# A fourth chunk of rotary angles reduced on TensorE, and three steps of the first units in another order

## The chip, the core and the metric

The kernel runs on one core of one Trainium2 chip. The core has TensorE (PE, matrix products into eight PSUM banks), VectorE (DVE), ScalarE (ACT), GpSimd (POOL) and SyncE (SP, which issues DMAs here); each works through its own queue of instructions in order, and semaphores tie the queues together. The metric is the device time of one launch in microseconds (us), the median of the runs. Before the change it is 1221.59 us over 3 runs (1221.35 to 1222.02).

## The reference, cut to what matters

One layer: cross attention with rotary positions over 64 sequences, then a mixture of experts. Only the head of it bears on the change: keys and queries are turned by cosine and sine of position times frequency.

```python
inv_freq = 1.0 / THETA ** (jnp.arange(0, HD, 2, dtype=jnp.float32) / HD)
freqs = pos.astype(jnp.float32)[:, None, :, None] * inv_freq
emb = jnp.concatenate((freqs, freqs), axis=-1)
return x * jnp.cos(emb) + _rotate_half(x) * jnp.sin(emb)
...
q = _rope(_rms_norm(layernorm(x) @ Wq.T), draft_position_ids)      # 16 heads of 128
k = _rope(_rms_norm(concat(ctx, x) @ Wk.T), full_position_ids)     # 4 key heads
probs = softmax(q @ k.T * SCALE); attn = probs @ v; x = x + tanh(g) * (attn @ Wo.T)
x = x + tanh(g2) * (top-2 of 8 experts + shared expert)(layernorm(x))
```

## The kernel before

The 4096 tokens are 32 tiles of 128 tokens (two sequences each). A unit of attention is one tile t and one key head g, n = 4t + g; `pair` in each engine's queue holds the eight units of two tiles, and the pairs run one after another. The first pair is written apart, since the tables of angles and the split weights are made beside it. The order of every engine's queue is the order of the calls in its block, written out by hand; nothing is scheduled.

**Tables of angles.** The angles are made in eight chunks of 128x512, `sincos[c]`, numbers 0 to 3 for context positions and 4 to 7 for token positions (X0 = 4, so X0 + 3 is 7). They are taken in the order 0, 4, 1, 5, 2, 6, 3, 7 (`CHUNKS`). A chunk passes through: position times frequency (VectorE, L1241); the number of whole turns by adding and taking away a rounding constant (`whole_turns` on ScalarE, L927 and L928, or `first_turns` on VectorE); taking the turns back out in three parts of 2 pi, either as three dependent VectorE operations (`turn_back`, L1261) or as four products with scaled identities on TensorE (`angle_left`, L1899 and L1901) that leave the angle in a PSUM bank; the clamp to just below pi (`clamp`, L1275, VectorE, which also reads the PSUM bank); and `tables` on ScalarE: absolute value (L934), sine (L935), cosine as the sine of pi/2 minus the absolute value (L936). `PE_ANGLES` lists the chunks that TensorE turns back, and `b_angle` their banks. The clamps add to the semaphore `angle_v` in the order of `CHUNKS`; each finished table adds to `sin_ready`, on which SP stores the chunk to `trig_scratch`.

**The first units beside it.** TensorE makes the first queries and keys and values (L1814, L1825) from unsplit weights, transposes turned keys and queries (`heads_T`, L1844, L1848), and forms the scores (L1859), for which it needs ScalarE's copy of the transposed queries (`queries_out`, L968) and VectorE's copy of the keys (`keys_out`, L1339). ScalarE takes the sums of squares (`query_squares` L962, `key_squares` L950), copies the values (L957), and forms the exponentials of the scores (L979) after a change of its function table (the load at L1062). GpSimd turns the sums of squares into scales and finishes queries and keys (L767 to L782). VectorE turns keys (`turn_keys`, L1317, L1319) and queries (L1331, L1333).

**The second context tile.** SP loads `ctx_raw` of tile 1 (`load_inputs(1, 1)`, L446) behind the last four loads of query and key weights. `context_hi(1, ...)` on ScalarE (L1002) copies it into `kv_in_hi`; it waits for that load alone. `context_lo(1, 1)` on VectorE takes the remainder later.

```python
            tables(2)
            tables(X0 + 2)
            tables(3)
            query_squares(1, 1)
...
                    if g == 0 and not end:
                        context_hi(t + 1, i + p, 1 - p)
```

Of the kernel before, what the change touches and what calls it, by code (L numbers as in the profile page):

```python
# [24 lines left out]
ALU = mybir.AluOpType  # L25
ACT = mybir.ActivationFunctionType
# [72 lines left out]
def flamingo(nc, x, ctxT, posx, posc, invf, g_xattn, g_ffn, q_w, k_w, wq, wkv, wo, wr, wg, wd, out):  # L99
    ctx = ExitStack()  # L100
    with ctx:
# [64 lines left out]
        def wkv_group(a, g):  # L166
# [56 lines left out]
        X0 = NCH // 2  # L223
        pos_f = sb("pos_f", [P, 2 * TILES], F32, stage_at)
        sincos = [sb(f"sincos{c}", [P, CH, 2, HALF], F32,
                     early_at if c in (0, X0) else stage_at if c == 2 else None) for c in range(NCH)]
# [94 lines left out]
        b_q, b_kv, b_qT, b_kT, b_sc, b_pT, b_aT, b_o = [  # L321
            bank(n) for n in ("b_q", "b_kv", "b_qT", "b_kT", "b_sc", "b_pT", "b_aT", "b_o")]
        b_count = b_table = b_kT
        b_angle = (b_sc, b_pT, b_aT)
        b_sg, b_shT, b_sT, b_sy = [b_q, b_kv], [b_qT, b_sc], [b_kT, b_o], [b_aT, b_pT]
        b_early = (b_q, b_kv, b_pT, b_aT), (b_qT, b_sc, b_pT, b_aT)
        b_gate, b_up, b_down = (b_q, b_kv), (b_kT, b_o), (b_sc, b_qT, b_aT, b_pT)
# [97 lines left out]

        CHUNKS = [c for n in range(X0) for c in (n, X0 + n)]
        ACT_TURNS = [0, X0, 1, X0 + 1, 3, X0 + 3]
        PE_ANGLES = [X0 + 1, 2, X0 + 2]
        turned_at, back_done = {}, {}


# [480 lines left out]
        def _(act):  # L912
# [4 lines left out]
            def step(ins):  # L917

                steps[0] += 1
                ins.then_inc(act_step, 1)  # L920
                act.wait_ge(act_step, steps[0])
# [8 lines left out]
            def tables(c):  # L930

                act.wait_ge(angle_v, CHUNKS.index(c) + 1)
                cos, sin = sincos[c][:, :, 0, :], sincos[c][:, :, 1, :]
                step(nc.scalar.activation(cos, sin, ACT.Abs))  # L934
                nc.scalar.activation(sin, sin, ACT.Sin)  # L935
                nc.scalar.activation(cos, cos, ACT.Sin, bias=half_pi[:], scale=-1.0).then_inc(sin_ready, 1)  # L936

# [115 lines left out]
            whole_turns(X0 + 3)  # L1053
            tables(2)
            tables(X0 + 2)
            tables(3)
            query_squares(1, 1)

# [5 lines left out]
            def pair(i, first, last, part):  # L1064
                for u in range(2 * KVH):
                    p, g = divmod(u, KVH)
# [22 lines left out]
                        split_hi(pieces[2 * u - 2:2 * u])  # L1089
                    if isinstance(i, int) and i == 1 and p == 0:  # L1090
                        split_hi(pieces[SPLITS + g:SPLITS + g + 1])
                    if g == 0 and not end:
                        context_hi(t + 1, i + p, 1 - p)
                    if g == 1 and not end:
                        normed_hi(t + 1, 1 - p)
# [129 lines left out]
        def _(dve):  # L1225
# [29 lines left out]
            def turn_back(*chunks):  # L1255
                for part in TWO_PI:
                    for c in chunks:
                        if part == TWO_PI[0]:
                            dve.wait_ge(turns_ready, ACT_TURNS.index(c) + 1)
                        turn, a = sincos[c][:, :, 0, :], sincos[c][:, :, 1, :]  # L1260
                        link(nc.vector.scalar_tensor_tensor(out=a, in0=turn, scalar=-part, in1=a, op0=ALU.mult,  # L1261
                                                            op1=ALU.add), len(chunks))
                        back_done[c] = steps[0]

            def clamp(*chunks):
                for c in chunks:
                    a = sincos[c][:, :, 1, :]
                    if c in PE_ANGLES:
                        n = PE_ANGLES.index(c)
                        dve.wait_ge(count_done, n + 1)  # L1270
                        left = b_angle[n][:].rearrange("p (t n) -> p t n", t=CH)
                    else:
                        dve.wait_ge(step_v, back_done[c])
                        left = a
                    nc.vector.tensor_scalar(a, left, PI_BELOW, -PI_BELOW, ALU.min, ALU.max).then_inc(angle_v, 1)  # L1275

            pieces = list(enumerate(split_pieces()))
# [198 lines left out]
                                    ALU.mult).then_inc(sin_w_ready, 1)  # L1476
            turn_queries(0, 0, 0, 0)
            clamp(2)
            turn_back(3)
            turn_keys(0, 0, 0)  # L1480
            clamp(X0 + 2, 3)
            turn_back(X0 + 3)
            clamp(X0 + 3)
            dve.wait_ge(st_trig_first, 16 * 2)
            keys_out(0, 0)
# [283 lines left out]
        def _(pe):  # L1769
# [138 lines left out]
            first_keys_values(0)  # L1908
            angle_left(1)
            angle_left(2)  # L1910
            first_queries(1)

            def shared_half(t, j, done):
# [368 lines left out]
```

## Time and profile before

| | us |
|---|---|
| median of 3 runs | 1221.59 |
| the profiled execution | 1223.99 |
| its span, first to last instruction | 1222.2 |
| TensorE busy | 1199.6 (98%) |
| VectorE busy | 1037.9 (85%) |
| GpSimd busy | 941.1 (77%) |
| ScalarE busy | 903.5 (74%) |
| chain that ended last | PE 92%, DVE 4%, ACT 3%, issue 1% |

Busy times are of one profiled execution, and a busy TensorE is not one at its peak. A row of a timeline has the start in us from the start of the span, the time taken, the engine, the line, the operation and the tiles; a bracket at its end tells how long the engine had been idle and what ended that. Buffer numbers are left out of the names there, so all eight chunks read `sincos`. A row of the view of stretches has from:to and length in us, the busy us of PE, PEld (weight loads), DVE, ACT and POOL with their instructions, the clock granted to TensorE as a share of 2.4 GHz, the busy share of the DMA engines, and GB/s.

### The profile page before, as it was taken

How to read it: one execution, taken by the hardware profiler on the slowest of the kernel's cores; microseconds unless marked ns; L12 is line 12 of the kernel's file. 1: busy time of each engine (PE TensorE's matmuls, PEld its weight loads, DVE VectorE, ACT ScalarE, POOL GpSimd, SP SyncE). 2: the span in 40 equal slices, each digit the busy share in tenths (PEclk: the TensorE clock that was granted, in tenths of full speed). 3: DMA queues.
4: the chain of work that ended last, by engine and by line, in shares of the span. 5: the costliest groups of instructions: out<-in, count | busy, mean ns of one | idle time of the engine just before them, and what ended most of it. 6: DMA issues, size and time to landing. Idle time of an engine off the chain costs nothing.

```text
span 1222.2 us, 31455 instructions
## 1 busy us (share of the span) xinstructions
PE 1199.6 (98%) x8765; PEld 1113.0 (91%) x8766; DVE 1037.9 (85%) x3014; ACT 903.5 (74%) x3774; POOL 941.1 (77%) x1124
## 2 busy tenths in 40 slices
PE   6899999999999999999999999999999999999999
PEld 3788999999999999999999999999999999999887
DVE  8788999999999999999989999988888777777554
ACT  7978787887888778887888877877777646666422
POOL 2778888888888888888888888888888525555585
PEclk9999999999999999999999999999999999999999
DMA  6634233332222222223333333332235636555485
GB/s 178 201 105 127 83 99 104 111 97 90 90 90 90 90 92 93 90 95 94 96 96 114 107 101 99 105 102 80 75 108 151 225 105 192 158 164 159 149 274 183
DMA packets 141079, 148.55 MB, mean 122 GB/s; under 512 B 13824, under 2 KB 124672, under 8 KB 140256
## 3 DMA queue, kind: packets, MB, share of 16 engines
q1 hardware_dynamic: 126096, 125.97, 34.2%
q0 software_dynamic: 6480, 17.77, 4.0%
q10 hardware_dynamic: 8448, 4.20, 1.2%
q8 instruction: 21, 0.34, 0.1%
q14 instruction: 34, 0.28, 0.1%
HBM read 66.93 MB, written 80.76 MB: 121 GB/s over the span
## 4 chain that ended last, share of the span: by engine, by line
PE 92%; DVE 4%; ACT 3%; issue 1%; DMA 0%; SPq 0%; DVEq 0%; ACTq 0%
PE b_kv L1801 14%; PE b_q L1787 14%; PE b_o L1885 13%; PE b_sc L1859 9%; PE b_aT L1874 9%; PE b_pT L1867 5%; PE b_qT L1848 4%; PE b_q L2121 3%; PE b_kv L2121 3%; PE b_kT L1844 2%; PE b_kT L2181 1%; PE b_o L2181 1%; PE b_kv L2181 1%; PE b_q L2181 1%; PE b_aT L2138 1%; PE b_pT L2138 1%
## 5 line engine op out<-in xcount | busy, mean ns | idle before, releaser
L1801 PE MATMUL b_kv<-w_group,kv_in_hi 128*128 128x256 f32 x992 | 204.9, 304 | 0.0
L979 ACT ACTIVATE probs<-b_sc,neg_max 128x128 f32<-128x128 f32 x512 | 180.6, 371 | 2.6 <-DVE neg_max L1343 2.1
L773 POOL TENSOR_TENSOR q_rot<-q_rot,q_sin 128x512 f32<-128x512 f32 x128 | 176.7, 1381 | 7.2 <-DVE q_sin L1333 2.4
L769 POOL TENSOR_TENSOR qk_r<-qk_me,minus_half 128x6 f32<-128x6 f32 x128 | 172.0, 1344 | 10.1
L1801 PEld LDWEIGHTS b_kv<-w_group,kv_in_hi 128*128 128x128 f32 x992 | 161.3, 190 | 7.3 <-issue 0.4
L1787 PE MATMUL b_q<-w_group,kv_in_hi 128*128 128x512 f32 x496 | 164.8, 413 | 0.4 <-DVE q_sin L1333 0.4
L1885 PE MATMUL b_o<-wo_hi,aT_hi 128*128 128x256 f32 x480 | 143.5, 299 | 0.3 <-DVE aT_lo L1357 0.3
L1859 PE MATMUL b_sc<-kT,qT 128*128 128x128 f32 x1024 | 136.3, 276 | 6.2 <-ACT qT L968 4.5
L776 POOL TENSOR_TENSOR q_rot<-q_rot,qk_r 128x512 f32<-128x512 f32 x128 | 133.7, 1044 | 10.0
L1801 PE MATMUL b_kv<-w_group,kv_in_lo 128*128 128x256 f32 x496 | 139.6, 282 | 0.0
L962 ACT ACTIVATE junk<-b_q 128x128 bf16<-128x128 f32 x512 | 134.0, 283 | 0.0
L1874 PE MATMUL b_aT<-pT,v 128*128 128x256 f32 x512 | 133.9, 384 | 0.0
L1859 PEld LDWEIGHTS b_sc<-kT,qT 128*128 128x128 f32 x1024 | 125.0, 191 | 8.8 <-issue 7.6
L1885 PE MATMUL b_o<-wo_lo,aT_hi 128*128 128x256 f32 x480 | 132.9, 277 | 0.0
L1885 PE MATMUL b_o<-wo_hi,aT_lo 128*128 128x256 f32 x480 | 132.7, 276 | 0.0
L973 ACT ACTIVATE pT<-b_pT 128x512 f32<-128x512 f32 x128 | 76.8, 600 | 69.6 <-PE b_pT L1867 67.6
L767 POOL TENSOR_TENSOR qk_me<-qk_ms,eps_rms 128x6 f32<-128x6 f32 x128 | 32.2, 252 | 108.6 <-ACT junk L950 108.4
L962 ACT ACTIVATION_READ_ACCUMULATOR junk<-b_q 128x1 f32 x512 | 111.2, 217 | 0.0
L1343 DVE TENSOR_REDUCE neg_max<-b_sc 128x4 f32<-128x512 f32 x128 | 88.0, 688 | 24.0 <-PE b_sc L1859 22.8
L979 ACT ACTIVATION_READ_ACCUMULATOR probs<-b_sc,neg_max 128x1 f32 x512 | 108.0, 211 | 0.0
L1874 PEld LDWEIGHTS b_aT<-pT,v 128*128 128x128 f32 x512 | 94.2, 189 | 15.0 <-issue 0.5
L782 POOL TENSOR_TENSOR k_rot<-k_rot,k_sin 128x256 f32<-128x256 f32 x128 | 94.6, 739 | 6.0 <-DVE k_sin L1319 4.3
(332 smaller groups left out, 3977.3 us busy)
## 6 DMA issues: line engine op xcount, KB each, us to landing
xs_scratch<-zeros SPq DMA_DIRECT2D x34, 1032.0 KB, 6.2
s_in<-xs_scratch SPq DMA_DIRECT2D x71, 129.0 KB
yT_scratch<-yT SPq DMA_DIRECT2D x32, 256.0 KB
routed<-ys_scratch SPq DMA_DIRECT2D x32, 256.0 KB, 4.3
w_hi_all<-w_scratch SPq DMA_DIRECT2D x3, 1536.0 KB, 14.4
x_in<-in_x SPq DMA_DIRECT2D x32, 128.0 KB, 2.3
ctx_raw<-in_ctxT SPq DMA_DIRECT2D x32, 128.0 KB, 2.5
trig_scratch<-sincos SPq DMA_DIRECT2D x8, 512.0 KB, 5.9
```

The costliest lines, as they stand in the source:

```text
L769: nc.gpsimd.tensor_tensor(qk_r[g % 2][:], qk_me[:], minus_half[:, 0:REP + NB], ALU.pow).then_inc(r_ready, 1)
L773: nc.gpsimd.tensor_tensor(q_rot[g % 2][:], q_rot[g % 2][:], q_sin[g % 2][:], ALU.add) \
L776: nc.gpsimd.tensor_tensor(q_rot[g % 2][:], q_rot[g % 2][:], qk_r[g % 2][:, 0:REP].unsqueeze(2).to_broadcast([P, REP, HD]), ALU.mult) \
L782: nc.gpsimd.tensor_tensor(k_rot[g % 2][:], k_rot[g % 2][:], k_sin[g % 2][:], ALU.add) \
L962: last = nc.scalar.activation(junk[:, h, :], b_q[:, h * HD:(h + 1) * HD], ACT.Square, scale=HD ** -0.5, accum_out=qk_ms[g % 2][:, h:h + 1])
L979: last = nc.scalar.activation(probs[:, j, :], b_sc[:, j * P:(j + 1) * P], ACT.Exp, bias=neg_max[g % 2][:, j:j + 1], accum_out=row_sum[g % ...
L1343: nc.vector.tensor_reduce(neg_max[g % 2][:], b_sc[:].rearrange("p (j n) -> p j n", j=REP), AX.X, ALU.max, negate=True).then_inc(max_ready, 1)
L1787: last = nc.tensor.matmul(b_q[:], kv_in[p][a][:, c, 1:3, :], wq_of(b, gg)[:, c, :], start=(c == 0 and (a, b) == PASSES[0]), stop=(c == DC ...
L1801: last = nc.tensor.matmul(b_kv[:, s * 2 * HD:(s + 1) * 2 * HD], kv_in[p][a][:, c, 2 * s:2 * s + 2, :], wkv_of(b, c)[:, g % KVH, :], start= ...
L1859: last = nc.tensor.matmul(b_sc[:, o:o + P], qT[:, s, 2 * j:2 * j + 2, :], kT[:, s, :], start=True, stop=True)
L1874: last = nc.tensor.matmul(b_aT[:, s * REP * S:(s + 1) * REP * S], v_s[g % KVH][:, s, :], pT[:, s, :], start=True, stop=True)
L1885: last = nc.tensor.matmul(b_o[:, 0:D], aT[a][:, h, :, :], wo_s[b][:, gg * REP + h, :], start=(gg == 0 and h == 0 and (a, b) == PASSES[0]), ...
```

## The change

Five edits. Chunk 3 joins the chunks that TensorE turns back, with bank `b_o`; its three VectorE operations go. `angle_left(3)` is put behind `angle_left(2)` and ahead of the queries of unit 1. On VectorE, the keys of unit 0 are turned right behind the clamp of chunk 2, and the clamp of chunk 3 comes behind the turning back of chunk 7. The absolute value of chunk 7 goes from ScalarE to VectorE. The context copy of tile 1 is taken out of unit 0 and put between the tables of chunks 6 and 3.

```diff
--- before.py
+++ after.py
@@ -321,7 +321,7 @@
         b_q, b_kv, b_qT, b_kT, b_sc, b_pT, b_aT, b_o = [
             bank(n) for n in ("b_q", "b_kv", "b_qT", "b_kT", "b_sc", "b_pT", "b_aT", "b_o")]
         b_count = b_table = b_kT
-        b_angle = (b_sc, b_pT, b_aT)
+        b_angle = (b_sc, b_pT, b_aT, b_o)
         b_sg, b_shT, b_sT, b_sy = [b_q, b_kv], [b_qT, b_sc], [b_kT, b_o], [b_aT, b_pT]
         b_early = (b_q, b_kv, b_pT, b_aT), (b_qT, b_sc, b_pT, b_aT)
         b_gate, b_up, b_down = (b_q, b_kv), (b_kT, b_o), (b_sc, b_qT, b_aT, b_pT)
@@ -425,7 +425,8 @@
 
         CHUNKS = [c for n in range(X0) for c in (n, X0 + n)]
         ACT_TURNS = [0, X0, 1, X0 + 1, 3, X0 + 3]
-        PE_ANGLES = [X0 + 1, 2, X0 + 2]
+        PE_ANGLES = [X0 + 1, 2, X0 + 2, 3]
+        DVE_ABS = [X0 + 3]
         turned_at, back_done = {}, {}
 
 
@@ -931,7 +932,8 @@
 
                 act.wait_ge(angle_v, CHUNKS.index(c) + 1)
                 cos, sin = sincos[c][:, :, 0, :], sincos[c][:, :, 1, :]
-                step(nc.scalar.activation(cos, sin, ACT.Abs))
+                if c not in DVE_ABS:
+                    step(nc.scalar.activation(cos, sin, ACT.Abs))
                 nc.scalar.activation(sin, sin, ACT.Sin)
                 nc.scalar.activation(cos, cos, ACT.Sin, bias=half_pi[:], scale=-1.0).then_inc(sin_ready, 1)
 
@@ -1053,6 +1055,7 @@
             whole_turns(X0 + 3)
             tables(2)
             tables(X0 + 2)
+            context_hi(1, 0, 1)
             tables(3)
             query_squares(1, 1)
 
@@ -1089,7 +1092,7 @@
                         split_hi(pieces[2 * u - 2:2 * u])
                     if isinstance(i, int) and i == 1 and p == 0:
                         split_hi(pieces[SPLITS + g:SPLITS + g + 1])
-                    if g == 0 and not end:
+                    if g == 0 and not (end or first and p == 0):
                         context_hi(t + 1, i + p, 1 - p)
                     if g == 1 and not end:
                         normed_hi(t + 1, 1 - p)
@@ -1272,6 +1275,9 @@
                     else:
                         dve.wait_ge(step_v, back_done[c])
                         left = a
+                    if c in DVE_ABS:
+                        nc.vector.scalar_tensor_tensor(out=sincos[c][:, :, 0, :], in0=left, scalar=-1.0, in1=left, op0=ALU.mult,
+                                                       op1=ALU.max)
                     nc.vector.tensor_scalar(a, left, PI_BELOW, -PI_BELOW, ALU.min, ALU.max).then_inc(angle_v, 1)
 
             pieces = list(enumerate(split_pieces()))
@@ -1476,10 +1482,10 @@
                                     ALU.mult).then_inc(sin_w_ready, 1)
             turn_queries(0, 0, 0, 0)
             clamp(2)
-            turn_back(3)
             turn_keys(0, 0, 0)
-            clamp(X0 + 2, 3)
+            clamp(X0 + 2)
             turn_back(X0 + 3)
+            clamp(3)
             clamp(X0 + 3)
             dve.wait_ge(st_trig_first, 16 * 2)
             keys_out(0, 0)
@@ -1908,6 +1914,7 @@
             first_keys_values(0)
             angle_left(1)
             angle_left(2)
+            angle_left(3)
             first_queries(1)
 
             def shared_half(t, j, done):
```

ScalarE, from the tables of chunk 2 to the change of function table; sincos_138, 142, 139, 143 are chunks 2, 6, 3, 7. Before:

```order
L936 ACTIVATE sincos_142<-sincos_142,half_pi 128x8x64
L934 ACTIVATE sincos_139<-sincos_139 128x8x64
L935 ACTIVATE sincos_139<-sincos_139 128x8x64
L936 ACTIVATE sincos_139<-sincos_139,half_pi 128x8x64
L962 ACTIVATE junk,qk_ms_107<-b_q 128x128 x4
L968 ACTIVATE qT<-b_qT 128x4x2x64
L950 ACTIVATE junk,qk_ms_107<-b_kv 128x128 x2
L934 ACTIVATE sincos_143<-sincos_143 128x8x64
L935 ACTIVATE sincos_143<-sincos_143 128x8x64
L936 ACTIVATE sincos_143<-sincos_143,half_pi 128x8x64
L957 ACTIVATE v_120<-b_kv 128x256
L1002 ACTIVATE kv_in_hi<-ctx_raw_96 128x2x2x64
```

ScalarE, the same stretch in the changed kernel:

```order
L938 ACTIVATE sincos_142<-sincos_142,half_pi 128x8x64
L1004 ACTIVATE kv_in_hi<-ctx_raw_96 128x2x2x64
L936 ACTIVATE sincos_139<-sincos_139 128x8x64
L937 ACTIVATE sincos_139<-sincos_139 128x8x64
L938 ACTIVATE sincos_139<-sincos_139,half_pi 128x8x64
L964 ACTIVATE junk,qk_ms_107<-b_q 128x128 x4
L970 ACTIVATE qT<-b_qT 128x4x2x64
L952 ACTIVATE junk,qk_ms_107<-b_kv 128x128 x2
L937 ACTIVATE sincos_143<-sincos_143 128x8x64
L938 ACTIVATE sincos_143<-sincos_143,half_pi 128x8x64
L959 ACTIVATE v_120<-b_kv 128x256
```

The context copy has moved ten instructions forward, ahead of the tables of chunk 3, and one absolute value of chunk 7 is gone.

VectorE, behind the turning of the first queries (`sincos_138<-b_pT` is the clamp of chunk 2). Before:

```order
L1275 TENSOR_SCALAR sincos_138<-b_pT 128x8x64
L1261 SCALAR_TENSOR_TENSOR sincos_139<-sincos_139 128x8x64 x3
L1317 SCALAR_TENSOR_TENSOR k_rot_115<-b_kv,qk_r_109,cos_w_85 128x128
L1319 SCALAR_TENSOR_TENSOR k_sin_117<-b_kv,qk_r_109,sin_w_87 128x128
L1317 SCALAR_TENSOR_TENSOR k_rot_115<-b_kv,qk_r_109,cos_w_85 128x128
L1319 SCALAR_TENSOR_TENSOR k_sin_117<-b_kv,qk_r_109,sin_w_87 128x128
L1275 TENSOR_SCALAR sincos_142<-b_aT 128x8x64
L1275 TENSOR_SCALAR sincos_139<-sincos_139 128x8x64
L1261 SCALAR_TENSOR_TENSOR sincos_143<-sincos_143 128x8x64 x3
L1275 TENSOR_SCALAR sincos_143<-sincos_143 128x8x64
```

VectorE, the same stretch in the changed kernel:

```order
L1281 TENSOR_SCALAR sincos_138<-b_pT 128x8x64
L1323 SCALAR_TENSOR_TENSOR k_rot_115<-b_kv,qk_r_109,cos_w_85 128x128
L1325 SCALAR_TENSOR_TENSOR k_sin_117<-b_kv,qk_r_109,sin_w_87 128x128
L1323 SCALAR_TENSOR_TENSOR k_rot_115<-b_kv,qk_r_109,cos_w_85 128x128
L1325 SCALAR_TENSOR_TENSOR k_sin_117<-b_kv,qk_r_109,sin_w_87 128x128
L1281 TENSOR_SCALAR sincos_142<-b_aT 128x8x64
L1264 SCALAR_TENSOR_TENSOR sincos_143<-sincos_143 128x8x64 x3
L1281 TENSOR_SCALAR sincos_139<-b_o 128x8x64
L1279 SCALAR_TENSOR_TENSOR sincos_143<-sincos_143 128x8x64
L1281 TENSOR_SCALAR sincos_143<-sincos_143 128x8x64
```

Three operations of chunk 3 are gone from in front of the keys' turn, and one on chunk 7 (its absolute value) is new.

## Rows read from the trace of the kernel before

**Rows 1.** Stretches, the steady loop: busy us of five engines, clock, DMA share, GB/s.

```profile
200.00:600.00 400.00, 400.00 (x3063) 376.80 (x3062) 365.27 (x1021) 321.44 (x1464) 343.95 (x386) 1.00 0.31 97
```

**Rows 2.** Timeline of TensorE, 21 to 43 us.

```profile
21.77 1.02 PE L1899 MATMUL b_aT<-sincos,ident 128*128 128x512 f32 x2
22.63 2.74 PE L1901 MATMUL b_aT<-sincos,back 128*128 128x512 f32 x6
25.21 1.88 PE L1814 MATMUL b_q<-wq_raw,kv_first 128*128 128x512 f32 x4
28.36 0.44 PE L1844 MATMUL b_kT<-ident,k_rot 128*128 128x128 f32 x2 [1.27 <-POOL k_rot L782]
...
33.50 1.49 PE L1859 MATMUL b_sc<-kT,qT 128*128 128x128 f32 x8 [2.53 <-ACT qT L968]
34.78 3.24 PE L1814 MATMUL b_q<-wq_raw,kv_first 128*128 128x512 f32 x4
...
39.59 0.38 PE L1844 MATMUL b_kT<-ident,k_rot 128*128 128x128 f32 x2
39.81 0.60 PE L1848 MATMUL b_qT<-ident,q_rot 128*128 128x128 f32 x4
41.43 1.13 PE L1859 MATMUL b_sc<-kT,qT 128*128 128x128 f32 x8 [1.02 <-ACT qT L968]
```

**Rows 3.** Stretches of the head, same columns.

```profile
34.10:37.50 3.40, 3.40 (x9) 1.85 (x8) 1.90 (x6) 3.35 (x6) 3.24 (x4) 0.50 1.01 297
...
41.40:58.00 16.60, 16.57 (x100) 14.49 (x101) 14.47 (x27) 15.65 (x59) 13.19 (x13) 1.00 0.47 151
```

**Rows 4.** The chain that ended last, in order: start, us, what.

```profile
37.75 1.40 ACT probs L979 x8
```

**Rows 5.** Timeline of ScalarE, 28 to 42 us.

```profile
28.13 0.63 ACT L934 ACTIVATE sincos<-sincos 128x512 f32<-128x512 f32 x1 [2.41 <-DVE sincos L1275]
...
29.95 0.61 ACT L934 ACTIVATE sincos<-sincos 128x512 f32<-128x512 f32 x1
...
33.72 0.67 ACT L934 ACTIVATE sincos<-sincos 128x512 f32<-128x512 f32 x1
34.42 0.63 ACT L935 ACTIVATE sincos<-sincos 128x512 f32<-128x512 f32 x1
...
35.57 0.36 ACT L957 ACTIVATE v<-b_kv 128x256 f32<-128x256 f32 x1
35.83 0.40 ACT L1002 ACTIVATE kv_in_hi<-ctx_raw 128x256 fp32r<-128x256 f32 x1
36.25 1.28 ACT L1062 ACT_TABLE_LOAD   x1
...
37.66 0.35 ACT L979 ACTIVATE probs<-b_sc,neg_max 128x128 f32<-128x128 f32 x1
...
40.63 0.66 ACT L968 ACTIVATE qT<-b_qT 128x512 f32<-128x512 f32 x1
```

**Rows 6.** Timeline of VectorE, 23 to 31 us.

```profile
23.25 3.09 DVE L1261 SCALAR_TENSOR_TENSOR sincos<-sincos 128x512 f32<-128x512 f32 x3
...
27.42 0.68 DVE L1275 TENSOR_SCALAR sincos<-b_aT 128x512 f32<-128x512 f32 x1
...
28.51 2.13 DVE L1261 SCALAR_TENSOR_TENSOR sincos<-sincos 128x512 f32<-128x512 f32 x3
```

**Rows 7.** Timeline of GpSimd: scales of unit 0, key sum of unit 1.

```profile
22.75 1.34 POOL L769 TENSOR_TENSOR qk_r<-qk_me,minus_half 128x6 f32<-128x6 f32 x1
...
37.95 0.72 POOL L782 TENSOR_TENSOR k_rot<-k_rot,k_sin 128x256 f32<-128x256 f32 x1
```

**Rows 8.** Timeline of SP: the issue of the second context tile.

```profile
25.24 0.67 SPq L446 DMA_DIRECT2D ctx_raw<-in_ctxT  x1
```

**Rows 9.** DMA issues, 25 to 25.9 us; last number: us to landing.

```profile
ctx_raw<-in_ctxT SPq DMA_DIRECT2D x1, 128.0 KB, 6.8
```

**Rows 10.** Line L446, first 5 us: the first context tile.

```profile
DMA to landing us min/median/max: 2.2/2.2/2.2
```

## Prediction, made before the changed kernel ran

> **What bounds the kernel now.** I read the stretches of the run first. In the steady loop TensorE is busy 400.00 of 400 us and its clock is full [rows 1]. What happens in the first 40 us can therefore reach the end in one way only: by the moment from which TensorE runs without a gap. The timeline of TensorE shows where that is [rows 2]. It waits 1.27 us at 28.36 for the first keys from GpSimd, 2.53 us at 33.50 and 1.02 us at 41.43, both times for ScalarE's copy of the transposed queries (qT). Behind the scores of the second unit at 41.43 it is busy 16.57 of 16.60 us [rows 3]. So the number to forecast is the shift of that 41.43, and every microsecond of it is a microsecond of the kernel.
>
> The chain of waits says what sets 41.43. Ahead of it there is no TensorE, only ScalarE, through the first exponentials at 37.75 in that view [rows 4]. The timeline of ScalarE gives its links [rows 5]: tables of chunk 6 from 28.13 (after an idle 2.41 us, for the clamp on VectorE), tables of chunk 3 from 29.95, sums of squares of unit 1, absolute value of chunk 7 at 33.72 and its sine at 34.42, values at 35.57, the context copy at 35.83, the load of the function table at 36.25, exponentials at 37.66, second qT at 40.63. The 2.41 us of idleness is what the reordered clamps can shorten.
>
> **The change, part by part.**
>
> VectorE, keys before the turning back. The three operations of chunk 3 (3.09 us at 23.25) stand before the keys' turn and the clamp of chunk 6 at 27.42 [rows 6]. Without them the keys can go once GpSimd has their scales, at 22.75 + 1.34 = 24.1 [rows 7], and take the 1.04 us that lie between the end of the three (26.34) and 27.42. The clamp of chunk 6 then needs TensorE's third block, whose last product ends at 22.63 + 2.74 = 25.37 [rows 2]. With its 0.68 us ScalarE can begin chunk 6 at about 26.1 instead of 28.13: 2.0 us earlier. Chunk 6 takes 29.95 - 28.13 = 1.82 us [rows 5], so ScalarE is free at 27.9.
>
> ScalarE, the context copy. It now stands there, and waits for `ctx_raw` of tile 1. SP issues that load at 25.24 [rows 8], and it lands 6.8 us later [rows 9], at 32.04. Nothing in the change comes ahead of that issue: the loads before it wait for chunks 0 and 4 and for weights, which are as before. So ScalarE, free at 27.9, stands for 4.1 us. In the kernel before, the copy ran at 35.83 and found its data there. Queued behind the waiting copy are the tables of chunk 3, the sums of squares of unit 1, the first qT, the tables of chunk 7, the values and the exponentials; for them wait GpSimd's scales of unit 1, VectorE's turn of its queries, and TensorE's first scores. The copy occupies 36.25 - 35.83 = 0.42 us at most, so the tables of chunk 3 begin at 32.04 + 0.4 = 32.45 against 29.95: +2.5 us. That is the large term. The sums of squares, the first qT and the first scores (33.50, now 36.0) take it over whole.
>
> The Trainium skill (DMA: Bandwidth & Descriptors, section Two DMAs through the same engine are not ordered) says that within one queue of one engine descriptors start in order, though their writes may finish out of order. By that rule the 128 KB stand behind the weights issued before them. The trace agrees: 6.8 us here, 2.2 us for the same transfer at the start, with little ahead of it [rows 9, 10].
>
> ScalarE, two things taken away behind that. The absolute value of chunk 7 frees 34.42 - 33.72 = 0.70 us. The context copy is gone from between values and table load; the load then waits for the end of the values' copy (35.57 + 0.36 = 35.93) instead of 36.23, which frees 0.30 us [rows 5]. Together: first exponentials at 37.66 + 2.5 - 0.70 - 0.30, a shift of +1.5 us.
>
> VectorE, the absolute value as a fourth operation on chunk 7, and the late clamp of chunk 3. TensorE's fourth block costs what the third did, 25.21 - 21.77 = 3.44 us [rows 2], and ends at 25.37 + 3.44 = 28.8. VectorE's three operations on chunk 7 take 2.13 us [rows 6] from 26.1, so it waits for the block and clamps chunk 3 until 29.5. The absolute value (0.7 us, as one of the three) and the last clamp end near 30.7. Cost zero: ScalarE wants chunk 3 at 32.45. If that cover is gone, chunk 3 can start at 29.5.
>
> TensorE, the fourth block. It pushes the queries of unit 1 to 28.65, and with their 1.88 us the first transposes to about 30.5 instead of 28.36 [rows 2]. The keys of unit 1 end near 33.0 instead of 31.0. All of it lies before the scores at 36.0. Cost zero; without cover 2.1 us, on qT.
>
> From the exponentials to 41.43 there are two ways. By ScalarE alone the second qT moves from 40.63 by +1.5, and the scores to 42.9. It needs the transposes of unit 1 done by 42.1. GpSimd's sum of its keys ran at 37.95 for 0.72 us [rows 7]; it hangs on the sums of squares and moves by 2.5, to end at 41.2, and the transposes take 40.41 - 39.59 = 0.82 us [rows 2]: 42.0, just in time. That holds with TensorE at full clock. Before, it was not: between 34.10 and 37.50 the granted clock was 0.50, so 1.2 GHz, after the idle 2.53 us [rows 3], and the queries of unit 2 took 3.24 us instead of the 1.88 of unit 1 at full clock [rows 2]. That slowness was covered. If it follows the scores again, the distance from scores to transposes stays at 39.59 - 33.50 = 6.09, they start at 42.1, end at 42.9, qT takes 0.66 and TensorE begins about 0.15 later: 43.7, a shift of +2.2. The idle time before the scores is now 3.0 us rather than 2.53, so a fall is no less likely, but TensorE worked longer just before it (until 33.0). I can't decide between the two ends and take the middle.
>
> The sum: +1.5 to +2.2, taken as +1.85 us. The profiled execution took 1223.99 (span 1222.2 and 1.8 around it), 2.4 above the median; the difference is laid on the median: 1221.59 + 1.85 = 1223.4.
>
> **The rivals.**
>
> (a) The load isn't late. If `ctx_raw` lands by 29.2, ScalarE copies it while it waits for the clamp of chunk 3, which ends at 29.5 instead of 29.95: -0.4. With -0.70 and -0.30 that is -1.4 us, 1220.2. The balance is zero for a landing at 30.5. For it: the first context tile took only 2.2 us [rows 10]. Against it: this very transfer took 6.8 [rows 9], and what is ahead of it is unchanged. [...]
>
> (b) Nothing much moves: a landing near 30.5, or losses and gains that meet elsewhere. 1221.6. It needs the load to be 1.5 us faster than in the trace.
>
> (c) Clearly slower: the fall of TensorE's clock comes later and lies on work that nothing covers. The place is behind the second scores, from 42.9 on. A stretch as long as the one before (3.4 us) at half speed costs 1.7 us of full-speed work [rows 3]: 1.5 + 1.7 = +3.2, 1224.8. It decides as soon as the low clock reaches past 42.9. For it: the idle time before the first scores is longer and ends 2.5 us later. Against it: before, the clock was back 4 us after TensorE resumed at 33.50; the same distance now gives 40.0.
>
> A fourth thought, that TensorE's extra block itself sets the pace, needs ScalarE's wait to vanish; then transposes at 30.5 and a chunk 3 at 29.5 would still be in time for qT at 32.3, so it belongs to (a).
>
> **How the numbers follow.** Forecast 0.67, (a) 0.12, (b) 0.08, (c) 0.13. A change of 0.2% (2.4 us) is about what this measurement can tell from none. The forecast's own range, with 0.4 us for run to run, (the three runs spread over 0.67) is 1222.7 to 1224.2; a fifth of it lies above 1224.0, so slower by over 0.2% gets 0.13 of it and all of (c): 0.26. Faster by over 0.2% (under 1219.2) needs more than (a): 0.03. Within 0.2%: 0.71. The range of 8 in 10 takes in (b), (c) and the upper edge of (a): 1220.6 to 1225.0.
>
> **What would show it.** In the profile after: ScalarE idle for about 4 us before the context copy, ended by the DMA of `ctx_raw`, at about 32.1; tables of chunk 6 at 26.1; the table load 1.5 us later than 36.25; TensorE idle some 3 us before scores at 36.0; second scores at 42.9 to 43.7, the upper end only if the granted clock is low over the queries of unit 2; no gap behind that. The forecast is wrong if the copy finds its data (a), if TensorE waits there for anything but qT, or if the shift at 41.43 doesn't reach the end.

## The result

| | before | changed |
|---|---|---|
| median, us (22 runs each) | 1222.03 | 1223.82 |
| lowest to highest | 1221.35 to 1223.24 | 1222.98 to 1225.38 |
| profiled execution, its span | 1223.99, 1222.2 | 1223.86, 1222.1 |
| second scores in the profile | 41.43 | 43.84 |

The ratio of changed to before is 1.0017 [1.0011, 1.0023]: 2.1 us slower by the ratio, 1.8 by the medians. The forecast was 1223.4, worked out as 1.85 us on top of 1221.59, the median of the first three runs; over 22 runs the median of the kernel before is 1222.03, and the forecast shift on top of that gives 1223.9.

ScalarE of the changed kernel, 26 to 44 us. The columns are as in [rows 5], whose rows these answer.

```profile
26.14 0.63 ACT L936 ACTIVATE sincos<-sincos 128x512 f32<-128x512 f32 x1 [0.41 <-DVE sincos L1281]
...
32.28 0.42 ACT L1004 ACTIVATE kv_in_hi<-ctx_raw 128x256 fp32r<-128x256 f32 x1 [4.22 <-DMA ctx_raw<-in_ctxT]
32.60 0.61 ACT L936 ACTIVATE sincos<-sincos 128x512 f32<-128x512 f32 x1
...
37.49 0.42 ACT L959 ACTIVATE v<-b_kv 128x256 f32<-128x256 f32 x1
37.93 1.28 ACT L1065 ACT_TABLE_LOAD   x1
...
43.10 0.60 ACT L970 ACTIVATE qT<-b_qT 128x512 f32<-128x512 f32 x1
```

Chunk 6 comes 2.0 us earlier than before. Then ScalarE stands for 4.22 us until the second context tile is there, and chunk 3 begins at 32.60 instead of 29.95. The table load is 1.68 us later than before: 2.65 lost at chunk 3, less what was taken away behind it.

TensorE of the changed kernel, answering to [rows 2].

```profile
25.22 1.02 PE L1905 MATMUL b_o<-sincos,ident 128*128 128x512 f32 x2
26.07 2.74 PE L1907 MATMUL b_o<-sincos,back 128*128 128x512 f32 x6
...
30.37 0.38 PE L1850 MATMUL b_kT<-ident,k_rot 128*128 128x128 f32 x2
...
36.14 1.13 PE L1865 MATMUL b_sc<-kT,qT 128*128 128x128 f32 x8 [3.23 <-ACT qT L970]
37.11 3.21 PE L1820 MATMUL b_q<-wq_raw,kv_first 128*128 128x512 f32 x4
...
42.25 0.38 PE L1850 MATMUL b_kT<-ident,k_rot 128*128 128x128 f32 x2
...
43.84 1.13 PE L1865 MATMUL b_sc<-kT,qT 128*128 128x128 f32 x8 [0.78 <-ACT qT L970]
```

The fourth block is the two rows on `b_o`. It ends at 28.8, and the transposes of unit 0 begin at 30.37 without a wait. TensorE then waits 3.23 us for qT. The queries of unit 2 again take 3.21 us, since the clock fell; it did so later than before. Stretches, columns as in [rows 3]:

```profile
34.10:37.50 3.40, 1.36 (x9) 1.19 (x10) 1.48 (x3) 3.40 (x17) 0.77 (x2) 1.00 1.11 335
37.50:41.00 3.50, 3.50 (x7) 1.68 (x6) 1.77 (x6) 3.47 (x15) 3.42 (x4) 0.51 1.14 340
...
41.00:43.80 2.80, 2.06 (x13) 1.62 (x11) 1.82 (x5) 2.28 (x14) 1.83 (x5) 1.00 1.16 342
...
44.50:60.00 15.50, 15.50 (x94) 13.41 (x93) 13.44 (x27) 14.52 (x56) 12.19 (x13) 1.00 0.25 83
```

Before, the stretch from 34.10 to 37.50 had the granted clock 0.50 (1.2 GHz); now it is the next one, and from 41.00 it is full (2.4 GHz). From 44.50 to 60 TensorE has no gap. Between 60 and 200 it is idle for 3.3 us, and for 3.4 us in the kernel before (136.71 and 136.62 us busy of 140), so the head's shift is carried along. The chain of waits of the changed kernel, cut to 25 to 46 us (start, us, what), names the cause in one line:

```profile
25.36 6.90 DMA ctx_raw<-in_ctxT
...
32.28 0.42 ACT kv_in_hi L1004
...
36.14 1.13 PE b_sc L1865 x8
37.27 3.04 PE b_q L1820 x4
...
43.84 1.13 PE b_sc L1865 x8
```

In the kernel before this part of the chain holds no DMA. Behind the first scores it now runs through TensorE at low clock, no longer through ScalarE's exponentials [rows 4].

**Why the two spans are equal though the kernel is slower.** I followed three operations that both kernels have: one on GpSimd near 90 us, one on TensorE near 990, and TensorE's last product. The timelines of the kernel before, with two pauses of VectorE near 1109 us:

```profile
90.55 1.04 POOL L776 TENSOR_TENSOR q_rot<-q_rot,qk_r 128x512 f32<-128x512 f32 x1
...
990.06 0.38 PE L2097 MATMUL b_kT<-ident,s_pair 128*1 128x128 f32 x2 [0.36 <-DVE s_pair L1667]
...
1108.66 0.29 DVE L1689 TENSOR_TENSOR s_hid<-s_silu,b_q 128x128 f32<-128x128 f32 x1 [0.69 <-issue]
...
1110.19 0.22 DVE L1700 CAST s_hT_lo<-s_hT_hi 64x128 fp32r<-64x128 f32 x1 [1.08 <-issue]
...
1219.21 0.28 PE L2210 MATMUL b_pT<-w_hi_all,gT_lo 96*128 96x256 f32 x1
```

Changed:

```profile
92.90 1.04 POOL L777 TENSOR_TENSOR q_rot<-q_rot,qk_r 128x512 f32<-128x512 f32 x1
...
991.91 0.38 PE L2104 MATMUL b_kT<-ident,s_pair 128*1 128x128 f32 x2 [0.36 <-DVE s_pair L1673]
...
1219.09 0.28 PE L2217 MATMUL b_pT<-w_hi_all,gT_lo 96*128 96x256 f32 x1
```

The shift is +2.41 at the second scores, +2.35 at 90 us, +1.85 at 990 us and -0.12 at the last product. So of the 2.41 about 0.6 are gone by 990 us, and another 2.0 between there and the end. In that last part VectorE of the kernel before pauses for 0.69 and 1.08 us with nothing in the profile that it waits for. Its profiled execution (1223.99) lies above the highest of its 22 timed runs (1223.24). So this one execution has a delay of its own, of nearly 2 us, late in it; its cause is open. For this question the spans can't be compared; the shift in the head and the timed ratio can.

### The profile page after: what moved, and what is told of

It reads as the page before. It is cut to its first block, busy times and chain, and to the rows that moved or that the text cites. A ratio compares the mean times of both kernels' runs of the same rounds, so it can differ in the third digit from the quotient of the medians.

```text
span 1222.1 us, 31468 instructions
## 1 busy us (share of the span) xinstructions
PE 1201.3 (98%) x8773; PEld 1114.1 (91%) x8774; DVE 1033.4 (85%) x3012; ACT 902.8 (74%) x3773; POOL 939.0 (77%) x1124
## 4 chain that ended last, share of the span: by engine, by line
PE 93%; DVE 3%; ACT 2%; SPq 1%; DMA 1%; issue 1%; DVEq 0%; ACTq 0%
PE b_kv L1807 14%; PE b_q L1793 14%; PE b_o L1891 13%; PE b_sc L1865 9%; PE b_aT L1880 9%; PE b_pT L1873 5%; PE b_qT L1854 4%; PE b_q L2128 3%; PE b_kv L2128 3%; PE b_kT L1850 2%; PE b_kT L2188 1%; PE b_o L2188 1%; PE b_kv L2188 1%; PE b_q L2188 1%; PE b_aT L2145 1%; PE b_pT L2145 1%
```

## The experiments

They ran in four groups, each on one chip with the kernel before beside it: e1 to e4 with before at 1224.39 us; e5, e6, e8 and e9 with 1224.32; the changed kernel again, e9 again and e10 with 1221.89; e10 again with 1224.15. So only ratios are compared across groups. Each ratio rests on 8 to 11 timed executions of the edited kernel, the first row's on 22.

| run | ratio to before, 95% | in us | second scores | shift at 90 us | clock low |
|---|---|---|---|---|---|
| the changed kernel | 1.0017 [1.0011, 1.0023] | +2.1 | 43.84 | +2.35 | yes |
| the same again | 1.0016 [1.0007, 1.0025] | +2.0 | 43.47 | +1.97 | partly |
| e1, copy back | 0.9995 [0.9985, 1.0004] | -0.6 | 40.53 | -0.76 | no |
| e2, only the copy moved | 1.0027 [1.0017, 1.0037] | +3.3 | 45.25 | +3.76 | yes |
| e3, load early | 0.9997 [0.9988, 1.0006] | -0.4 | 41.06 | -0.01 | no |
| e4, TensorE fed | 1.0020 [1.0009, 1.0030] | +2.4 | 43.36 | +2.04 | no |
| e5, only the absolute value | 0.9999 [0.9989, 1.0008] | -0.1 | 41.22 | -0.25 | yes |
| e6, no fourth block, copy back | 1.0005 [0.9996, 1.0014] | +0.6 | 42.14 | +0.64 | yes |
| e8, e6 and output weights late | 1.0003 [0.9994, 1.0012] | +0.4 | 42.43 | +0.92 | yes |
| e9, e1 and output weights late | 0.9993 [0.9984, 1.0002] | -0.9 | 40.38 | -1.09 | no |
| e9 again | 0.9992 [0.9983, 1.0001] | -1.0 | 40.69 | -0.77 | no |
| e10, e3 and output weights late | 0.9992 [0.9983, 1.0001] | -1.0 | 40.05 | -1.28 | no |
| e10 again | 0.9988 [0.9979, 0.9998] | -1.5 | 40.96 | -0.37 | no |

The us are (ratio - 1) times before; the shift is of the row at 90.55 above. Over the thirteen rows shift and timed difference agree within 0.6 us, but for e10's second run (1.1): the head of the kernel accounts for what is timed.

The column on the clock is of one profiled execution. The mean granted clock of every timed execution is on record too; 1.000 leaves room for about 1.2 us at half clock in a span of 1222 us. It was 1.000 in all 44 executions of e9 and e10 and in 10 of 11 of e1, in none of the 22 of e6 and e8, and 0.997 or 0.998 in all nine of e2. Of the changed kernel's first 22, seven had 1.000 and took 1223.5 us in the mean, the other 15 took 1224.2. In the kernel before the two kinds differ by 0.3 us at most in each group, in either direction: there the low clock is covered.

One more thing varies between executions of the same kernel: the moment at which TensorE first reaches full clock (see the last section). The first two products of its first angle block tell: 1.02 us at full clock, 1.47 in the kernel before and 1.46 in the changed one, so this pair can be compared; 1.02 in e1 and in e9, but 1.91 in e3, e6 and e8, and 1.92 in e2.

**e1_copy_back**: the changed kernel with the context copy where it was.

```diff
-            context_hi(1, 0, 1)
             tables(3)
...
-                    if g == 0 and not (end or first and p == 0):
+                    if g == 0 and not end:
                         context_hi(t + 1, i + p, 1 - p)
```

> The changed kernel with the context copy of tile 1 put back into unit 0, behind the values; all else of the change stays. Theory (the copy stands on ScalarE for its load): ScalarE doesn't wait behind the tables of chunk 6; chunk 3 starts when its clamp is done, about 29.6 us instead of 29.95 in the kernel before (-0.4), and the absolute value taken away gives -0.7: second scores at 40.3 us, time 1.1 us under the kernel before, 2.9 us under the changed one. Rival (the fourth TensorE block, or the moved clamps, cost the time): the idle time at 28 to 32 us stays in another form and the time stays at +1.8 us over before.

The loss is gone: 3.3 us earlier at the second scores than the changed kernel, and the ratio interval lies wholly below that of the changed kernel. TensorE, then ScalarE, then VectorE of it:

```profile
33.25 1.13 PE L1864 MATMUL b_sc<-kT,qT 128*128 128x128 f32 x8 [1.04 <-ACT qT L970]
34.22 1.88 PE L1819 MATMUL b_q<-wq_raw,kv_first 128*128 128x512 f32 x4
...
40.53 1.13 PE L1864 MATMUL b_sc<-kT,qT 128*128 128x128 f32 x8 [1.17 <-ACT qT L970]
```

```profile
29.69 0.63 ACT L936 ACTIVATE sincos<-sincos 128x512 f32<-128x512 f32 x1 [1.75 <-DVE sincos L1280]
...
34.87 0.46 ACT L1004 ACTIVATE kv_in_hi<-ctx_raw 128x256 fp32r<-128x256 f32 x1
...
45.62 0.60 ACT L997 ACTIVATE aT_first<-b_aT 128x512 f32<-128x512 f32 x1 [0.75 <-DMA trig_scratch<-sincos]
```

```profile
30.51 0.42 DVE L1344 COPY kT<-b_kT 128x256 f32<-128x256 f32 x1
```

The copy waits for nothing at 34.87. Two things are new. The queries of unit 2 take 1.88 us rather than 3.24: the clock didn't fall. And with everything earlier, ScalarE is early at `aT_first` (L997), which waits on the stores of the tables. Against the kernel before, chunk 3 starts only 0.26 us earlier (29.69 against 29.95), though chunk 6 starts 2.1 earlier: the clamp of chunk 3 now stands behind the turning back of chunk 7 on VectorE, and ScalarE waits 1.75 us for it. The rest of the 0.90 us at the second scores is the absolute value.

**e2_copy_only**: the kernel before with nothing changed but the copy's place (the reverse of that diff).

> The kernel before with only the context copy moved in front of the tables of chunk 3. Theory: chunk 3 starts at 32.6 instead of 29.95 us (+2.65), the place behind the values gives back 0.3, second scores at 43.8 us with TensorE's low clock over the queries of unit 2: time 2.4 us over the kernel before (+1.6 to +2.6), so this one edit is more than the whole change. Rival (the TensorE block or the clamps cost it): no difference from before.

The copy alone costs 3.3 us (2.4 were expected), and the second scores came at 45.25 (43.8 were expected). By the ratios that is 1.2 us more than the whole change costs, with intervals that overlap. ScalarE, then TensorE, of it:

```profile
32.81 0.42 ACT L1002 ACTIVATE kv_in_hi<-ctx_raw 128x256 fp32r<-128x256 f32 x1 [2.69 <-DMA ctx_raw<-in_ctxT]
```

```profile
36.67 2.05 PE L1860 MATMUL b_sc<-kT,qT 128*128 128x128 f32 x8 [5.63 <-ACT qT L968]
38.52 3.58 PE L1815 MATMUL b_q<-wq_raw,kv_first 128*128 128x512 f32 x4
```

ScalarE's wait is shorter than in the changed kernel (2.69 against 4.22), since it arrives later, but the landing sets the same moment. What differs is TensorE: without its fourth block it is idle for 5.63 us, and the clock is low for twice as long. In the stretches, with the same columns:

```profile
35.20:41.80 6.60, 5.13 (x12) 3.22 (x13) 3.01 (x7) 6.54 (x25) 4.46 (x6) 0.50 1.09 327
```

The second scores are 1.41 us later than in the changed kernel. Of these 0.53 are there when the copy starts (32.81 against 32.28: the load took 7.4 us here), and 0.9 come from the first scores, which take 2.05 us at low clock instead of 1.13. So the other parts of the change don't add to the loss. The fourth block, which keeps TensorE busy until 28.8, is the likely cause of the shorter low stretch; e2 lacks the other parts too, so this pair doesn't show it alone.

**e3_load_early**: the changed kernel, with tile 1's two loads issued ahead of the last four weight loads.

```diff
+            load_inputs(1, 1)
             sp.wait_ge(ld_rest, 32)
             for g in range(2, KVH):
...
-            load_inputs(1, 1)
```

> The changed kernel with the loads of the second tile (x_in and ctx_raw of tile 1) issued before the last four weight loads instead of behind them. Theory: issued at about 20.3 us it lands near 26, ScalarE finds it at 27.9, chunk 3 starts at 29.6; -0.4 for that, -0.7 for the absolute value, -0.3 for the copy gone from behind the values: second scores at 40.0 us, time 1.4 us under the kernel before, 3.2 under the changed one. The weights land 1 us later and nobody waits. Rival (it is the order on ScalarE, not the landing): still +1.8 us. Second rival: queries of unit 2 wait for their weights, seen as TensorE idle ended by the DMA of wq_raw.

The copy stays where the change put it and loses its wait; the loss is gone too. ScalarE:

```profile
28.84 0.40 ACT L1004 ACTIVATE kv_in_hi<-ctx_raw 128x256 fp32r<-128x256 f32 x1
30.53 0.63 ACT L936 ACTIVATE sincos<-sincos 128x512 f32<-128x512 f32 x1 [1.29 <-DVE sincos L1281]
...
46.50 0.60 ACT L997 ACTIVATE aT_first<-b_aT 128x512 f32<-128x512 f32 x1 [1.12 <-DMA trig_scratch<-sincos]
```

So it is the wait, not the copy's 0.4 us nor its place. The second scores were expected at 40.0 and came at 41.06: TensorE reached its first full clock late in this execution (1.91 us for the first two products); the fourth block began at 26.10 instead of 25.22, and chunk 3 at 30.53 instead of 29.6. Of the 0.37 us gained at the second scores nothing is left at 90 us (-0.01): the wait for `trig_scratch`, 1.12 us here, takes most of it (e10 lacks the wait, and gains 0.26 over that distance).

**e4_pe_fed**: the changed kernel, with three products of 128x512 that nothing reads, on TensorE where it would wait.

```diff
                         first_keys_values(1)
+                        pe.wait_ge(angle_v, 5)
+                        for m in range(3):
+                            nc.tensor.matmul(b_pT[:], ident[:], wq_raw[:, 0, 0:512], start=True, stop=True)
```

> The changed kernel with three more 128x512 products of constants and raw weights on TensorE, into bank b_pT (unused results), between the keys of unit 1 and the first scores, where TensorE stood idle 3.2 us. Theory: they end near 35.7 us and delay nothing; the granted clock stays at 1.00 over the queries of unit 2, which take 1.9 us instead of 3.2; second scores come when ScalarE's chain allows, 41.43 + 1.67 = 43.1 instead of 43.84 us: time 0.7 us under the changed kernel. Rival (the low clock was covered as in the kernel before): no difference from the changed kernel, +1.8 us over before.

TensorE of it:

```profile
32.90 2.74 PE L1966 MATMUL b_pT<-wq_raw,ident 128*128 128x512 f32 x6
36.39 1.13 PE L1865 MATMUL b_sc<-kT,qT 128*128 128x128 f32 x8 [0.75 <-ACT qT L970]
37.35 1.88 PE L1820 MATMUL b_q<-wq_raw,kv_first 128*128 128x512 f32 x4
...
43.36 1.13 PE L1865 MATMUL b_sc<-kT,qT 128*128 128x128 f32 x8 [0.86 <-ACT qT L970]
```

The clock stays full, and from first to second scores it is 6.97 us instead of 7.70. So the low clock costs the changed kernel 0.7 us there, close to the 0.8 between the two ends of the forecast (42.9 and 43.7). As `ctx_raw` landed 0.24 us later in this run, 0.48 is left at the second scores, and the time (+2.4 us) shows none of it, against the 0.7 us under the changed kernel that were expected: too small for this measurement. The changed kernel's own timed executions agree with 0.7 us (the seven at full clock against the other 15).

**e5_abs_only**: the kernel before, with the absolute value of chunk 7 on VectorE (`DVE_ABS` as in the change).

> The kernel before with one edit: the absolute value of chunk 7 is taken by VectorE (behind the turning back, ahead of the clamp) and no longer by ScalarE. Theory: 34.42 - 33.72 = 0.70 us leave ScalarE's chain, VectorE has the time; second scores at 40.7 instead of 41.4 us, time 0.7 us under before. Rival (VectorE's extra 0.7 us delays the copy of the first keys, from 31.3 to 31.9 us, and with it the scores): ScalarE's qT ends only at 33.35, so no delay; if it counts, no gain at all.

No difference in the time, where 0.7 us were expected. ScalarE's table load came 0.6 us earlier, nearly as worked out, but the second scores only 0.2: TensorE's low clock, covered before, was laid bare. (TensorE's idle time before them is 0.78 us instead of 1.02, as in the changed kernel: that is the way from its own transposes through ScalarE's copy, and ScalarE is not late.) It was granted 0.50 over this stretch:

```profile
33.60:36.90 3.30, 3.30 (x10) 2.46 (x11) 1.91 (x6) 3.28 (x8) 2.76 (x3) 0.50 1.00 299
```

**e6_dve_chunk3**: the changed kernel with the copy back and without TensorE's fourth block; VectorE turns chunk 3 back, behind the keys and the clamp of chunk 6.

```diff
-        PE_ANGLES = [X0 + 1, 2, X0 + 2, 3]
+        PE_ANGLES = [X0 + 1, 2, X0 + 2]
...
             clamp(X0 + 2)
-            turn_back(X0 + 3)
+            turn_back(3)
             clamp(3)
+            turn_back(X0 + 3)
...
-            angle_left(3)
```

> The changed kernel with the context copy back in unit 0 and without the fourth TensorE block: VectorE turns chunk 3 back again, but behind the keys' turn and the clamp of chunk 6, and clamps it before it turns chunk 7. Theory (the late clamp of chunk 3 behind TensorE's block holds ScalarE in e1_copy_back for 1.75 us): chunk 3 starts at 28.8 to 29.3 us instead of 29.7, second scores at 39.7 to 40.2 us, time 1.2 to 1.8 us under before, 0.3 to 0.8 under e1. Rival (ScalarE's wait for the last table store before the first attention output, 45.6 us in e1, gives it back): second scores earlier, time as in e1. Second rival: without TensorE's block its clock falls after the idle time and takes 0.7 us.

**e8_dve_chunk3_wo_late**: the same, with the first load of the output weights behind the stores of the tables.

```diff
-            load_wo(0)
             sp.wait_ge(st_trig_first, 16 * 2)
...
                 store_trig(c)
+            load_wo(0)
             load_wo(1)
```

> e6_dve_chunk3 with the load of the first half of the output weights (1 MB) issued behind the stores of the tables instead of ahead of them. Theory (those stores are late because of that load, and ScalarE waits 0.75 us and more for them at 45.6): the last store lands near 41 us instead of 45.2, no wait there, and time 1.8 us under before. Rival: that wait is off the path, TensorE runs without a gap there in e1, so the time is that of e6. Risk for both: the weights land too late for the first output product at 46 to 47 us, seen as TensorE idle ended by the DMA of wo_raw.

Against e1, e6 lacks the fourth block, and VectorE has three operations on chunk 3 more, which stand with its clamp ahead of the turning back of chunk 7. TensorE of e6, then VectorE, and a stretch:

```profile
33.57 1.16 PE L1865 MATMUL b_sc<-kT,qT 128*128 128x128 f32 x8 [3.44 <-DVE kT L1344]
35.30 3.58 PE L1820 MATMUL b_q<-wq_raw,kv_first 128*128 128x512 f32 x4 [0.56 <-DVE q_sin L1338]
...
42.14 1.13 PE L1865 MATMUL b_sc<-kT,qT 128*128 128x128 f32 x8 [0.78 <-ACT qT L970]
```

```profile
33.10 0.42 DVE L1344 COPY kT<-b_kT 128x256 f32<-128x256 f32 x1
```

```profile
35.60:38.90 3.30, 3.30 (x5) 1.24 (x4) 1.96 (x7) 2.54 (x10) 3.14 (x5) 0.50 1.06 319
```

The theory for both failed: second scores expected at 39.7 to 40.2 us came at 42.14 and 42.43, and a gain of 1.2 to 1.8 us in the time came as +0.6 and +0.4. Chunk 3 did not reach ScalarE earlier (29.61 against 29.69 in e1), and two other things got worse. VectorE, with chunk 3 to turn back, copies the keys at 33.10 instead of 30.51, so that the first scores wait for kT, and finishes the queries of unit 1 later; the queries of unit 2 begin 1.08 us later than in e1 (35.30 against 34.22). And TensorE, idle for 3.44 us before the first scores instead of 1.04, falls to half clock: those queries take 3.58 us instead of 1.88. The second scores are 1.6 us later than in e1, and 2.1 later in e8 than in e9.

So the exchange, fourth block against three operations on VectorE, is worth 1.6 to 2.1 us in the profile once ScalarE doesn't wait. How much of it is the clock and how much VectorE's queue isn't separated. A part is neither: e6 and e8 reached the first full clock late, e1 and e9 early. Against the second run of e9, which was nearly as late (1.73 us for the first two products, second scores at 40.69), e6 and e8 are 1.5 and 1.7 us later. In the time the difference of the two ratios is 1.2 us for each pair (1.0005 against 0.9995, 1.0003 against 0.9993), with intervals that overlap.

**e9_copy_back_wo_late**: e1 with that same move of the output weights.

> e1_copy_back with the same move of the output weights' load. Theory: as e1 in the head, second scores at 40.3 to 40.5 us, the wait at 45.6 gone, time 1.1 us under before; against e8 it shows what the fourth TensorE block costs or gives with the copy out of the way: 0.3 to 0.8 us slower than e8. Rival: the block keeps TensorE's clock up, then e9 is the faster of the two.

**e9_again**: the same kernel in another group.

> The changed kernel with the context copy back in unit 0 and the output weights' first load behind the stores of the tables, a second time. My theory: second scores at 40.4 to 41.0 us, no wait for ctx_raw or trig_scratch, a time 0.7 to 1.3 us under before, as the first run's 0.9993. Rival (its first result was chance): ratio of 1.0000 or above.

**changed_again**: the changed kernel, unedited.

> The changed kernel once more, unedited, beside the kernel before, on the chip of the experiments. My theory: ScalarE again waits about 4 us for ctx_raw, the second scores stand near 43.8 us of the profile, and the time is 1.5 to 2.5 us above before (ratio 1.0012 to 1.002). Rival (what the first pair of chips' numbers showed is chance or belongs to one chip): ratio under 1.0005 with the wait in the profile all the same.

**e10_load_early_wo_late**: e3 with that move of the output weights, a version that might beat both.

> The changed kernel with both reorderings of SP's loads: tile 1's x_in and ctx_raw ahead of the last four weight loads, and the first load of the output weights behind the stores of the tables. My theory (waiting for ctx_raw is what the change lost, and its other parts save): no wait at the copy, none for trig_scratch at aT_first, no fall of TensorE's clock between the first and second scores, second scores at 40.2 to 41.0 us against 41.43 before and 43.84 in the changed kernel, and a time 0.5 to 1.2 us under before. Rival (queue order only trades places: what comes early pushes the weights later, and units 1 and 2 wait for weights): a wait of TensorE or VectorE for weights of 0.5 us or more behind the second scores, and a time at or above before.

**e10_again**: the same kernel.

> The changed kernel with both reorderings of SP's loads, a second time, to tell whether it is faster than the kernel before. My theory: second scores at 40.0 to 40.8 us of the profile against 41.43, and a time 0.7 to 1.4 us under before, as the first run's 0.9992. Rival (the first result was chance): ratio of 1.0000 or above.

In e9 and in e10 the wait for `trig_scratch` is gone. e9 was to be 0.3 to 0.8 us slower than e8; it is the faster one, as its rival said. From second scores to the row at 90 us it is 49.08 us in e9 and 49.22 in e10, against 49.26 in e1, 49.48 in e3 and 49.12 in the kernel before. The gain, 0.2 to 0.3 us, is too small to be timed by itself. ScalarE of e10:

```profile
27.68 0.40 ACT L1004 ACTIVATE kv_in_hi<-ctx_raw 128x256 fp32r<-128x256 f32 x1
29.52 0.63 ACT L936 ACTIVATE sincos<-sincos 128x512 f32<-128x512 f32 x1 [1.44 <-DVE sincos L1281]
...
44.45 0.60 ACT L997 ACTIVATE aT_first<-b_aT 128x512 f32<-128x512 f32 x1
```

e10 came to 0.9992 and 0.9988, 1.0 and 1.5 us below before; the second interval excludes 1. It has the lowest ratios of all the versions, about 3 us below the changed kernel; from e9 the intervals don't tell it. The first interval of e10 and both of e9 just include 1, but the four agree in sign and nearly in size. The rival of e10, that the weights come too late for units 1 and 2, did not occur: none of the four engines waits for a DMA from 40 to 120 us. The changed kernel, repeated, was slower again by the same 0.16%.

## Why the prediction was right

By its own steps:

- **Keys' turn and chunk 6.** 24.1 and 26.1 were worked out; 24.22 and 26.14 came. It frees ScalarE earlier and brings nothing by itself, as ScalarE then stands at the copy. (The prediction reads the chain ahead of 41.43 as ScalarE alone. The view has VectorE in it from 20.3 to 28.1 us, with the turning back of chunk 3 and the clamps; the sum does use that part.)
- **The copy waits for `ctx_raw`.** Landing worked out for 32.04; it was 25.36 + 6.90 = 32.26, and the wait 4.22 us instead of 4.1. e1 and e3 show that this wait is the loss, by two ways that share no edit: one moves the copy, the other the load. Rivals (a) and (b) needed a landing by 30.5. The first scores, expected at 36.0, came at 36.14, after an idle 3.23 instead of 3.0. VectorE's three operations on chunk 7 took 2.85 us instead of the 2.13 in the sum, but ended with the fourth block, so the clamp of chunk 3 was done at 29.6, as worked out, and under cover.
- **The two things taken away behind it.** Table load expected 1.5 us later, measured 1.68; the 0.2 is the later landing. Of the 0.70 for the absolute value e5 shows 0.6 at the table load, of which 0.2 reach the second scores when it stands alone.
- **The clock.** Of the two ends (42.9 at full clock, 43.7 at low) the second came in the profile, at 43.84. The transposes began at 42.25 instead of 42.1, held up by TensorE at low clock and not by GpSimd, whose key sum ran at 40.58 for 0.72 us and ended at 41.30. e4, with the clock kept full, takes 0.7 us off the distance between the scores. Rival (c), low clock beyond the second scores, did not come: it was full again from 41, though that is 1 us later than the 40.0 that the prediction took from the kernel before.
- **The end.** The second scores' shift of 2.41 is the time's +1.8 to +2.1. That the forecast's 1.85 lies nearer to the time than to the profile is in part luck. It was the middle, for want of a decision on the clock, and single executions of the changed kernel fall on either side. Of the shift, 0.53 us are lost slowly between 90 and 960 us (2.35 to 1.82 on the same GpSimd operation, unit by unit). It sinks by 0.3 to 0.5 in ten of the thirteen profiles against this one profile of before, and by less than 0.1 in those of e1, e4 and e5. So it goes with the single execution, that of before among them, and not with the change.

**What the forecast put at zero and isn't zero.** "TensorE, the fourth block ... Cost zero" held in the changed kernel. But the block keeps TensorE busy until 28.8, and where ScalarE doesn't wait (e1, e3, e9, e10) the clock then doesn't fall in the head of the profile. Where VectorE turns chunk 3 back instead (e6, e8), the second scores come 1.6 to 2.1 us later. I had weighed only whether the block delays something, not what its work does for the clock, nor what VectorE's queue is spared.

The runs don't separate these two. In e6 the first scores waited for kT, which VectorE copied behind its three added operations; had kT been there, TensorE would have waited for qT until about 33.2, still some 3 us. That is an estimate from the rows, and it speaks for the clock. A kernel with VectorE's order of e1 and TensorE fed by other work wasn't run. The size of the other parts, one by one, isn't resolved either.

## What to carry to other kernels

A copy moved earlier in an in-order queue is as early as its load: look up the landing of its data in the DMA view before moving it, and move the load ahead with it, or leave both. When one wait takes all the gain, the other parts of a change may still be good: undo the suspected part alone before judging the whole (here that took 2.1 us above before to 0.6 below, the latter not resolved by itself). Where differences are a thousandth, follow one operation that both kernels have through the two profiles, and don't compare spans.

## What the runs showed of the hardware

**The first full clock comes at different moments in the same kernel.** The two products of TensorE's first angle block take 1.02 us at full clock, as those of the fourth block do above. The timeline of TensorE, first run and second run of e10:

```profile
12.63 1.13 PE L1905 MATMUL b_sc<-sincos,ident 128*128 128x512 f32 x2
```

```profile
12.76 1.92 PE L1905 MATMUL b_sc<-sincos,ident 128*128 128x512 f32 x2
```

In the second they run at half speed throughout, in the first hardly at all; its second scores are 0.91 us later, with not one instruction different. The view of stretches shows the granted clock as 1.00 there in both, so only the durations of the products tell. The Trainium skill (TensorE: Matmul & The Clock Gate, section The HAM clock gate) says too that the same kernel can rise to full clock at another moment in each run; the two traces agree. In the profile a difference of under 1 us between two kernels must be read against this. For the two runs of e9 (1.02 and 1.73 us) it is 0.31 us.

**When a load of 128 KB lands depends on what is queued ahead of it.** `ctx_raw` landed 6.9 us after issue in the changed kernel, 7.4 in e2, and 3.7 in e10 where four weight loads stood behind it rather than ahead; the first tile took 2.2 [rows 10].

**The same three VectorE operations** (subtraction of the turns, 128x512) took 3.09 and 2.13 us before [rows 6] and 2.85 for chunk 7 in the changed kernel. In the kernel before, one of the first three took 1.65 us while GpSimd ran a sum of two 128x512 tiles beside it (at 24.06 us, for 1.73; the same sum took 1.27 in the changed kernel, where VectorE turned keys from a PSUM bank then). From 28.51 GpSimd was idle, and each of the three took about 0.7. No run was made to separate this, so that the two engines slow each other here is likely but not shown.
